# ELU of four layers written as relu(x) - relu(1 - exp(x)), in a graph attention and mixture-of-experts kernel

## The reference

```python
def gat_layer(x, adj, W, a_self, a_neigh, b):
    feat = jnp.einsum('nf,hfo->hno', x, W)
    e = attn_self[:, :, None] + attn_neigh[:, None, :]
    e = jax.nn.leaky_relu(e, 0.2) + MASK_VAL * (1.0 - adj)[None, :, :]
    alpha = jax.nn.softmax(e, axis=-1)
    out = jnp.einsum('hnm,hmo->hno', alpha, feat) + b[:, None, :]
    out = jnp.transpose(out, (1, 0, 2)).reshape(out.shape[1], -1)
    return jax.nn.elu(out)
...
x = x + jnp.tanh(g_xattn[0]) * gat(gat(ctx_512))
x = x + jnp.tanh(g_ffn[0]) * moe(layernorm(x))
```

## Time and profile before

| | us |
|---|---|
| median of 3 runs | 446.31 (446.15 to 446.85) |
| the profiled execution's own time | 445.5 |
| its span in the trace | 443.7 |
| TensorE busy | 395.6 (89%) |
| VectorE busy | 257.2 (58%) |
| ScalarE busy | 205.5 (46%) |
| GpSimd busy | 90.5 (20%) |

### The profile page before, as it was taken

The page is one execution under the profiler, slowest core; times in us unless marked ns, Lnnn a source line. Parts: engine busy times, 40 slices in busy tenths (PEclk is TensorE's granted clock), DMA queues, the critical chain, the costliest instruction groups (busy, mean ns, idle before and its releaser), DMA issues.

```text
span 443.7 us, 7225 instructions
## 1 busy us (share of the span) xinstructions
PE 395.6 (89%) x2295; PEld 289.1 (65%) x2296; DVE 257.2 (58%) x814; ACT 205.5 (46%) x519; POOL 90.5 (20%) x100
## 2 busy tenths in 40 slices
PE   3877787787988999997999999999999999999991
PEld 2445464555765878776888886666667676766660
DVE  3799999899887784785474424343333333433330
ACT  4597999999854668420120213232232323232320
POOL 6656140001000022121312000212121212121221
PEclk9998999999998999998999999999999999999997
DMA  6199999100000001000698300122212222221212
GB/s 172 27 353 343 339 354 429 60 1 1 1 1 1 2 7 67 1 24 27 242 429 347 88 2 24 26 36 38 36 38 39 35 46 33 39 36 24 24 12 24
DMA packets 22988, 42.48 MB, mean 96 GB/s; under 512 B 1968, under 2 KB 20976, under 8 KB 21680
## 3 DMA queue, kind: packets, MB, share of 16 engines
q1 hardware_dynamic: 17632, 35.76, 23.3%
q0 software_dynamic: 4080, 5.18, 7.4%
q10 hardware_dynamic: 1248, 1.18, 0.8%
HBM read 24.81 MB, written 17.31 MB: 95 GB/s over the span
## 4 chain that ended last, share of the span: by engine, by line
PE 59%; DVE 19%; ACT 14%; POOL 3%; issue 2%; DMA 2%; POOLq 0%; DVEq 0%
PE ps_z L749 13%; PE ps_o L775 11%; PE ps_gu L749 9%; ACT weights L843 6%; PE ps_pt L605 5%; PE ps_z L598 5%; DVE weights L1041 5%; PE ps_gu L598 4%; DVE weights L1036 3%; ACT weights L834 3%; ACT weights L849 3%; PE ps_pt L765 3%; PE ps_gu L605 2%; DVE hidden L1094 1%; DVE gate_silu L1091 1%
## 5 line engine op out<-in xcount | busy, mean ns | idle before, releaser
L439 POOL DMA_INDIRECT out<-y_sb,tile_in x23 | 35.9, 1559 | 166.1 <-DVE y_sb L1280 163.0
L843 ACT ACTIVATE weights<-weights 128x256 f32<-128x256 f32 x128 | 64.3, 536 | 0.1
L749 PE MATMUL ps_z<-weights,tile_t 128*128 x184 | 63.2, 486 | 0.0
L775 PE MATMUL ps_o<-weights,hidden 128*128 x230 | 53.5, 380 | 0.9 <-ACT hidden L950 0.9
L1091 DVE SCALAR_TENSOR_TENSOR gate_silu<-gate_tanh,ps_z 128x256 f32<-128x256 f32 x66 | 24.5, 371 | 49.5 <-ACT gate_tanh L935 36.2
L517 PE MATMUL ps_pt<-ident,weights 128*128 128x128 f32 x256 | 35.4, 284 | 15.6 <-ACT weights L849 15.2
L749 PEld LDWEIGHTS ps_z<-weights,tile_t 128*128 128x128 f32 x184 | 33.2, 190 | 23.2 <-issue 22.0
L775 PEld LDWEIGHTS ps_o<-weights,hidden 128*128 128x128 f32 x230 | 43.6, 190 | 7.0 <-issue 1.1
L935 ACT ACTIVATE gate_tanh<-ps_gu 128x256 f32<-128x256 f32 x23 | 8.8, 383 | 80.5 <-PE ps_gu L749 80.5
L517 PEld LDWEIGHTS ps_pt<-ident,weights 128*128 128x128 f32 x256 | 29.9, 147 | 22.6 <-issue 21.8
L1036 DVE SCALAR_TENSOR_TENSOR weights<-weights 128x1024 f32<-128x1024 f32 x32 | 39.0, 1219 | 9.1 <-ACT weights L834 5.6
(11 more groups left out here) (192 smaller groups left out, 618.4 us busy)
## 6 DMA issues: line engine op xcount, KB each, us to landing
weights<-w_experts SPq DMA_DIRECT2D x8, 1920.0 KB, 14.1
slots<-pad_row SPq DMA_DIRECT2D x9, 1188.0 KB, 13.5
weights<-w_experts SPq DMA_DIRECT2D x1, 3840.0 KB, 14.5
tile_in<-slots SPq DMA_DIRECT2D x23, 132.0 KB, 2.1
out<-y_sb ACTq DMA_DIRECT2D x4, 256.0 KB, 2.2
weights<-x SPq DMA_DIRECT2D x2, 256.0 KB, 4.4
x_in<-x SPq DMA_DIRECT2D x2, 256.0 KB, 5.3
out<-y_sb,tile_in POOLq DMA_INDIRECT x23, 3.8
```

The costliest lines, as they stand in the source:

```text
L439: pool.indirect_dma_start(out=out, out_offset=bass.IndirectOffsetOnAxis(ap=tile_in[:, slot, ID_COL:ID_COL + 1].bitcast(U32), axis=0), in_= ...
L749: mm = pe.matmul(ps_chunk[c][:, 0:2 * cw], tile_t[:, r % 2, k, :], weights[:, bass.ds(off + (k * GU + 2 * c0), 2 * cw)], start=(k == 0), s ...
L775: mm = pe.matmul(ps_o[:, 0:D], hid_t[:, r % 2, i, :], weights[:, bass.ds(off + (KC * GU + i * D), D)], start=(i == 0), stop=(i == IC - 1))
L843: ins = act.activation(v, v, ACT.Exp, bias=neg_max[:, w % AHEAD, i:i + 1], scale=-1.0, accum_out=sums[:, L % PAIR, s:s + 1])
```

## The change

For the layers in `FULL_ELU`, which works out as L = 4, 5, 6 and 7, ScalarE takes over nearly all of the ELU. Beside each exponential it writes `elu` = relu(att + b) (new L866), then it waits for its own last instruction (`elu_step`) and rewrites `att_exp` in place as relu(1 - exp), 512 columns wide (new L870). VectorE's two instructions of `divide` are left out, with the wait behind them, and `end_elu` is one subtraction (new L1084) in place of one two-operation instruction.

```diff
+FULL_ELU = tuple(L for L in range(STREAM) if UNITS * (L + 1) >= step_after(0, UNITS))
...
                 act.wait_ge(o_read, L + 1)
                 for quad in range(QUADS):
                     ins = act.activation(att_exp[:, quad, :], att[:, quad, :], ACT.Exp, bias=bias_col(0, ORDER[L][1], quad))
+                    if L in FULL_ELU:
+                        ins = act.activation(elu[L % PAIR][:, quad, :], att[:, quad, :], ACT.Relu, bias=bias_col(0, ORDER[L][1], quad))
+                if L in FULL_ELU:
+                    ins.then_inc(elu_step, 1)
+                    act.wait_ge(elu_step, FULL_ELU.index(L) + 1)
+                    ins = act.activation(att_exp.rearrange("p a n -> p (a n)"), att_exp.rearrange("p a n -> p (a n)"), ACT.Relu,
+                                         scale=-1.0, bias=1.0)
                 ins.then_inc(exp_ready, 1)
...
                 dve.tensor_tensor(att, ps_o.rearrange("p (a n) -> p a n", a=QUADS), invb, ALU.mult).then_inc(o_read, 1)
+                if L in FULL_ELU:
+                    return
                 dve.wait_ge(o_read, L + 1)
...
                 dst, done = (h0_t[n], h0_ready) if layer == 0 else (elu[c], h1_ready)
+                if L in FULL_ELU:
+                    dve.tensor_tensor(dst, elu[c], att_exp, ALU.subtract).then_inc(done, 1)
+                    return
```

More of the change, by code:

```diff
@@ L231, in build @@
         o_ready, o_read, exp_ready = sem("o_ready"), sem("o_read"), sem("exp_ready")
+        elu_step = sem("elu_step")
         sums_inverted, invb_turned, invb_copied = sem("sums_inverted"), sem("invb_turned"), sem("invb_copied")
```

## The result

| | before | after |
|---|---|---|
| median, us | 446.23 (20 runs) | 449.85 (20 runs) |
| lowest to highest, us | 444.15 to 448.01 | 447.01 to 451.23 |
| the profiled execution's own time, us | 445.5 | 448.48 |
| its span, us | 443.7 | 446.7 |
| ScalarE busy, us | 205.5 | 211.0 |

The ratio of after to before is 1.0071, with a 95% interval of 1.0054 to 1.0089: 3.2 us slower, with 2.4 to 4.0 as the interval. The forecast was 449.4, in a range of 448.4 to 451.2.

The account below looks back on a forecast made before the run. The prediction took a chain of waits as the bound, 59% TensorE, 19% VectorE and 14% ScalarE. Layer costs 0 + 0.27 + 1.43 + 1.36 = 3.06 us gave 449.4 us against the median of 446.31, range 448.4 to 451.2.

Parts of the forecast that it names:

- The price on ScalarE: ELU on ScalarE: att_exp and the next ScalarE instruction are both ready 1.43 us later per layer.
- L = 4, 0: ELU of layer 4: the delay is hidden, with 0.43 us of cover before TensorE wants the bank; cost 0.
- L = 5, +0.27: ELU of layer 5: end_elu 1.01 us later, 0.74 absorbed by idle time before place's third instruction, 0.27 us stays.
- L = 6, +1.43: ELU of layer 6: TensorE's turn already waits for the ps_pt copy, so all 1.43 us adds to the path.
- The saved VectorE time: VectorE at layer 6: the saved time lies before 1.69 us of waiting for att_exp and buys nothing.
- L = 7, +1.36: ELU of layer 7: end_elu, place, GpSimd's transfers, power and normalise all come 1.36 us later.
- The sum: Whole kernel: costs of the four layers add to 3.06 us, giving 449.4 us against the median, 0.7% slower.
- The extra fall of the clock: Rival, behind TensorE's new pauses at L = 6 or 7: clock falls once more, 1.7 us, 451.1 us; chance 0.11.
- The prediction's reading of the clock: TensorE's clock: full speed up to 140 us, a fall at 142 to 144, a second behind the pause before normalise.
- The fall at 142: Rival, TensorE at 138 to 146: shifted work could avoid this fall, paying 1.7 us; one or both falls fewer, chance 0.05.
- VectorE's relief: Rival, VectorE at L = 6 and 7: 0.77 us removed at each counts, ScalarE's work hidden, 444.8 us; chance 0.03.

Follow-up runs that it names:

- e1: Changed kernel with the new ELU kept only at layers L = 4 and 5; ratio to the kernel before 0.9977 (0.9955 to 0.9999).
- e2: Changed kernel with the new ELU kept only at layer L = 6; ratio to the kernel before 0.9999 (0.9972 to 1.0026).
- e7: Changed kernel with each 256-column Relu executed a second time into an unread tile; ratio to the kernel before 1.0104 (1.0076 to 1.0131).
- e8: Changed kernel without the 512-column Relu and ScalarE's wait for itself; ratio to the kernel before 1.0013 (0.9988 to 1.0039).
- e9: The kernel before, unchanged, run and traced once more; median 446.01 us, ratio 1.0008 (0.9987 to 1.0029).
- e10: The changed kernel, run and traced once more; median 448.72 us, ratio to the kernel before 1.0073 (1.0046 to 1.0101).
- e3: Changed kernel with the new ELU kept only at layer L = 7; ratio to the kernel before 1.0006 (0.9977 to 1.0035).
- e6: Changed kernel with GpSimd's power of graph 3 ahead of its four row transfers; median 445.27 us, ratio to the kernel before 0.9979.
- e5: Kernel before with GpSimd's power of graph 3 ahead of its four row transfers; median 441.04 us, ratio 0.9901 (0.9874 to 0.9929).
- e4: Changed kernel with the copy of ps_pt ahead of the ELU on ScalarE at L = 4, 5 and 6; ratio to the kernel before 1.0074.

## Why the prediction was right

- **The price on ScalarE.** Spacing of 0.40 as taken; the wait for itself 0.04 where I took 0.03; the wide Relu 0.63 where I took 0.60 from the 512-column copy. The copy at L = 6 and the subtraction behind `att_exp` both start 1.46 us later after the first exponential, in place of 1.43.
- **L = 4, 0.** Right (a is 32.75 with the new ELU in e1 and with the old one in e2), and safer than argued: I named TensorE's wish for the bank as the limit (0.43 us), but e7 shows that behind it there is VectorE's product to wait for.
- **L = 5, +0.27.** The mechanism came out as worked out: the third instruction of `place` has no idle time left. It starts 3.40 us after the first exponential, against 3.06 before, so the cost is 0.34 rather than 0.27; e8 gives 0.33 and e1 0.32. That b differs by just 0.27 between the first two traces is luck, since b of the kernel before was 26.13 in e9. In one pair of sums (e10) nothing of it is seen.
- **L = 6, +1.43.** Measured +1.47 (c), alone too (e2). The saved VectorE time did lie in front of a longer wait, 4.05 us.
- **L = 7, +1.36.** Measured +1.39 (d), alone too (e3). That GpSimd's transfers carried the delay was right for the kernel as it is, but e6 shows that they weren't needed for it.
- **The sum.** 3.06 expected; 3.13 in the stretches, 3.2 (2.4 to 4.0) by the ratio. That span and median both came so close is partly luck: exp4 and a cancelled in the one pair of executions, both tails had a fall of the clock, and the clock moves a single run by more than a layer's ELU.
- **The rivals.** The extra fall of the clock behind the new pauses at L = 6 and 7 happened in the traces of neither the change nor its repetition, but it did in e7. The prediction's reading of the clock had a hole: it has TensorE at full speed up to 140 and counts two falls, but in the trace of before the clock had also fallen between 38 and 44 (0.67, 0.50, 0.98). The fall at 142 was indeed missing in the changed kernel's first trace, and the one in the tail in e2 and e3, so falls come and go from run to run, which I had taken for a property of the kernel. VectorE's relief bought nothing that the stretches show: at L = 6 and 7 the cost is ScalarE's full price. No run took the two instructions off VectorE alone.

## What to carry to other kernels

Moving work between two engines of similar speed is decided by who waits at that place: here 0.74 us less on VectorE was worth nothing, since VectorE then waited for ScalarE, and 1.46 us more on ScalarE cost from 0 to 1.46 us, depending on the cover behind it. Where an engine pauses on a chain of several engines, look at what stands ahead of the needed instruction in the last queue without being needed; here that was worth 1% for one line moved, a good third of it because the clock then did not fall. And when an effect of 1 us is buried in runs that scatter by 4, compare stretches between fixed events of the traces, not totals.

## What the hardware showed that I had not expected

The granted clock is a lottery within one kernel. TensorE paused for 3.1 us before `normalise` in nine of the twelve traces, all but those of e5, e6 and e7. The clock fell to the lower level behind this pause in six (before, after, e1, e4, e9, e10) and did not in three (e2, e3, e8). Behind the pause of 1.98 or 1.99 us at 138 to 143 us it fell in nine traces of twelve, and one kernel shows both outcomes: in the changed kernel's first trace the clock held at 142, in e10 it fell.

What a fall costs depends on where it comes. In the tail it is 1.1 to 1.9 us (240.64 to 241.02 in the six traces without a fall behind `normalise`, 242.12 to 242.55 in the six with one), in a 1.5 to 1.8 us, in c of e7 1.6 us, and in d of e7 nothing, since TensorE had to wait there anyway. That such falls make up most of the way from 444 to 448 us over which the runs of the unchanged kernel scatter is likely from the slope of 2.3 us per 0.01 of clock, but no run shows it directly.
